# Grouped expert rows in eight slots of 256 and three of 128, instead of eleven of 256

## What is computed

```python
macro_scores = sigmoid(xf @ macro_w)                 # 2048 x 4 groups
mv, mi = topk_normalized(macro_scores, 1)            # one group per row
micro_scores = sigmoid(einsum('td,gde->tge', xf, micro_w))
uv, ui = topk_normalized(micro_scores, 2)            # both experts of the group
w = (macro_full[:, :, None] * micro_full).reshape(T, 8)
gate = silu(einsum('td,edf->tef', xf, gate_w))       # d 256 -> f 512
up = einsum('td,edf->tef', xf, up_w)
out = einsum('te,tef,efd->td', w, gate * up, down_w)
x = x + out
```

## Time and profile before

| | us |
|---|---|
| median of 3 runs (1137.84 to 1138.3) | 1138.0 |
| profiled execution | 1138.74 |
| its span | 1137.0 |
| PE busy | 1035.9 (91%) |
| DVE busy | 783.1 (69%) |
| ACT busy | 692.4 (61%) |
| POOL busy | 565.8 (50%) |
| first h_tb matmul of the experts | at 940.8 |
| last scatter issued | at 1130.4 |

### The profile page before, as it was taken

One profiled execution on the slowest core, in us unless ns is written; L12 is line 12 of the kernel. 1 busy time (PEld: TensorE's weight loads), 2 busy tenths in 40 slices (PEclk: granted clock), 3 DMA queues, 4 the chain that ended last, 5 costly groups with the idle time before them and its releaser, 6 DMA issues. The chain is left out here.

```text
span 1137.0 us, 29115 instructions
## 1 busy us (share of the span) xinstructions
PE 1035.9 (91%) x10375; PEld 759.2 (67%) x10376; DVE 783.1 (69%) x2175; ACT 692.4 (61%) x1297; POOL 565.8 (50%) x685
## 2 busy tenths in 40 slices
PE   6999999999999999984699997898888858999995
PEld 3666777777777777773388884445454447888885
DVE  5887887788778877878734327877777774555452
ACT  6888876787668876757554335476756634334331
POOL 4678644666556553301467826266766432333312
PEclk9999999999999999995799998999999978999998
DMA  8633333343344334307746553534444221111200
GB/s 262 165 85 94 85 77 76 75 88 85 55 103 95 81 80 92 74 16 267 242 153 197 149 126 131 191 97 131 132 123 141 85 98 34 30 34 26 33 10 11
DMA packets 124382, 117.25 MB, mean 103 GB/s; under 512 B 47840, under 2 KB 104416, under 8 KB 124128
## 3 DMA queue, kind: packets, MB, share of 16 engines
q1 hardware_dynamic: 116960, 106.32, 33.5%
q0 software_dynamic: 7296, 9.25, 4.8%
HBM read 59.89 MB, written 21.82 MB: 72 GB/s over the span
## 5 line engine op out<-in xcount | busy, mean ns | idle before, releaser
L810 DVE TENSOR_TENSOR e_t_lo<-et,e_t_hi 128x512 f16<-128x512 f32 x256 | 176.7, 690 | 45.7 <-ACT e_t_hi L697 43.4
L704 ACT ACTIVATE e<-masked,neg_max 128x512 f32<-128x512 f32 x256 | 184.4, 720 | 37.6 <-DVE neg_max L836 35.0
L836 DVE CUSTOM_DVE_ANT_0 masked<-sc,mask_bias 128x512 f32<-128x512 f32 x256 | 175.5, 686 | 31.0 <-issue 26.5
L697 ACT ACTIVATE e_t_hi<-et 128x512 f16<-128x512 f32 x256 | 151.6, 592 | 71.4 <-PE et L581 70.1
L581 PEld LDWEIGHTS et<-ident,e 128*128 128x128 f32 x1024 | 124.5, 140 | 56.7 <-issue 8.7
L581 PE MATMUL et<-ident,e 128*128 128x128 f32 x1024 | 154.4, 273 | 1.0 <-ACT e L704 0.8
L2317 ACT ACTIVATE d_e<-d_st 128x384 f32<-128x384 f32 (+1 forms) x192 | 94.0, 526 | 42.9 <-PE d_st L2461 38.4
L74 PE MATMUL ob<-v_hi,e_t_hi 128*128 128x65 f16 x1024 | 119.0, 193 | 1.2 <-issue 1.2
L75 PE MATMUL ob<-v_lo,e_t_hi 128*128 128x65 f16 x1024 | 119.2, 193 | 0.0
L76 PE MATMUL ob<-v_hi,e_t_lo 128*128 128x65 f16 x1024 | 118.4, 193 | 0.0
L74 PE MATMUL h_hb<-h_xt_hi,experts_hi 128*128 128x256 f16 x352 | 96.8, 275 | 2.1 <-DVE h_xt_lo L2694 1.5
(11 more groups left out here) (504 smaller groups left out, 2847.7 us busy)
## 6 DMA issues: line engine op xcount, KB each, us to landing
kk<-nat_k SPq DMA_DIRECT2D x64, 256.0 KB, 3.5
raw<-in_fc SPq DMA_DIRECT2D x16, 1024.0 KB, 7.6
qq<-nat_q SPq DMA_DIRECT2D x64, 128.0 KB, 2.6
qk<-scratch_stack SPq DMA_DIRECT2D x64, 128.0 KB
scratch_stack<-kq_hi SPq DMA_DIRECT2D x16, 256.0 KB, 2.8
scratch_stack<-kq_lo SPq DMA_DIRECT2D x16, 256.0 KB, 3.0
d_expert_raw<-in_gate_w SPq DMA_DIRECT2D x8, 512.0 KB, 3.7
d_expert_raw<-in_up_w SPq DMA_DIRECT2D x8, 512.0 KB, 3.8
```

Of the source, the lines that this page charges most:

```text
L697: nc.scalar.activation(e_t[u % NBUF].hi[:], et[u % 2][:], ACT.Copy).then_inc(turned_hi, 1)
L704: nc.scalar.activation(e[u % NBUF][:], masked[u % NBUF][:], ACT.Exp, bias=neg_max[:, g % 2, j:j + 1], scale=-1.0).then_inc(exp_ok, 1)
L810: nc.vector.tensor_tensor(e_t[u % NBUF].lo[:], et[u % 2][:], e_t[u % NBUF].hi[:], ALU.subtract).then_inc(turned_lo, 1)
L836: nc.vector.tensor_tensor_reduce(masked[u % NBUF][:], sc[j % 2][:], mask_bias[g // PAIRS % 2][:, j % QT, :], -SCALE0, 3e38, ALU.add, ALU.m ...
```

## The change

Eleven slots stay eleven, but only slots 0 to 7 hold 256 rows (`FULL1` = 8); slots 8, 9 and 10 hold 128. `HALF_TILES`, the number of lists of 128 rows, is 2 * 8 + 3 = 19 instead of 22. A group's rows fill pairs of halves, and a remainder of at most 128 rows goes to a single half; where the pairs are nine, the ninth takes two of the single slots. The search works this out on DVE. In slots 8 to 10 every tile, matmul, activation, gather and scatter is for 128 rows.

```diff
-HALF_TILES = TILES1 * TILE // P
+FULL1 = B * S // TILE
+TILES1 = FULL1 + GROUPS1 - 1
+HALF_TILES = 2 * FULL1 + GROUPS1 - 1
...
-            step_done(dve, nc.vector.tensor_tensor(lower, full.rearrange("p a b -> p (a b)").unsqueeze(1).to_broadcast([P, GROUPS1, GROUPS1 * THRESHOLDS]),
...
-            step_done(dve, nc.vector.tensor_reduce(first_tile, lower, AX.X, ALU.add))
...
+            step_done(dve, nc.vector.tensor_reduce(counts, full.rearrange("p g (k t) -> p k g t", k=2), AX.X, ALU.add))
+            step_done(dve, nc.vector.tensor_tensor(counts[:, SINGLE, :], counts[:, SINGLE, :], counts[:, PAIRED, :], ALU.subtract))
...
+            step_done(dve, nc.vector.tensor_reduce(starts.rearrange("p a k -> p (a k)"), lower, AX.X, ALU.add))
+            pair_start, pair_end = (starts[:, i:i + GROUPS1, PAIRED] for i in range(2))
+            ahead(nc.vector.tensor_scalar(overfull, starts[:, GROUPS1, PAIRED:PAIRED + 1], float(B * S + TILE), float(TILE), ALU.is_ge, ALU.mult))
...
+            step_done(dve, nc.vector.tensor_tensor(over, place, pair_end.unsqueeze(1).to_broadcast([P, NT, GROUPS1]), ALU.is_ge))
...
+            step_done(dve, nc.vector.tensor_tensor(over, over, move.unsqueeze(1).to_broadcast([P, NT, GROUPS1]), ALU.mult))
+            step_done(dve, nc.vector.tensor_tensor(place, place, over, ALU.add))
...
+def halves_of(j):
+
+    return 1 if isinstance(j, int) and j >= FULL1 else 2
...
-            with eng.Fori(0, TILES1 // 2 - 1) as m:
+            with eng.Fori(0, FULL1 // 2 - 1) as m:
...
+            for j in range(FULL1 - 1, TILES1):
+                first(j, j % 2)
+                if j + 1 < TILES1:
+                    turn(j + 1, (j + 1) % 2)
+                tail(j - 1, (j - 1) % 2)
+            tail(TILES1 - 1, (TILES1 - 1) % 2)
...
-                        pool.wait_ge(stored, 32 * j)
+                        pool.wait_ge(stored, 16 * half_at(j))
                         pool.sem_inc(res_free, 1)
-                    for n in range(2):
...
+                    for n in range(halves_of(j)):
...
-                                mm = three_products(pe, hb[g % 2][:, which, :], weights(base, expert * EXPERT_COLS + start + c * FF1 + f * P, P),
-                                                    (xt[i].hi[:, c, :], xt[i].lo[:, c, :]), c == 0, c == DT - 1)
+                                mm = three_products(pe, hb[g % 2][:, which, rows_of], weights(base, expert * EXPERT_COLS + start + c * FF1 + f * P, P),
+                                                    (xt[i].hi[:, c, rows_of], xt[i].lo[:, c, rows_of]), c == 0, c == DT - 1)
```

More of the change, by code:

```diff
@@ L1927, in __init__ @@
         parts, weights = first.take([NT, PER_GROUP, GROUPS1]), first.take([NT, PER_GROUP])
-        full, lower = first.take([GROUPS1, THRESHOLDS]), first.take([GROUPS1, GROUPS1 * THRESHOLDS])
-        first_tile = first.take([GROUPS1])
+        full, counts = first.take([GROUPS1, 2 * THRESHOLDS]), first.take([2, GROUPS1])
+        lower, starts = first.take([2 * (GROUPS1 + 1), GROUPS1]), first.take([GROUPS1 + 1, 2])
+        overfull, fourth, single_at, move = first.take([1]), first.take([GROUPS1]), first.take([GROUPS1]), first.take([GROUPS1])
+        over = first.take([NT, GROUPS1])
         past, tile_group = first.take([TILES1, GROUPS1 - 1]), first.take([TILES1])
+        first_single, past_single = first.take([GROUPS1 - 1]), first.take([TILES1 - FULL1, GROUPS1 - 1])
+        single_group, in_pair = first.take([TILES1 - FULL1]), first.take([TILES1 - FULL1])
         place_at, low_digit, high_digit = (first.take([NT], I32) for _ in range(3))
@@ L1939, in __init__ @@
         ones, tri, zeros = third.take([P], F16), third.take([P], F16), third.take([NT + 1, GROUPS1], F16)
-        order, thresholds, tiles = third.take([GROUPS1]), third.take([THRESHOLDS]), third.take([TILES1])
-        before = third.take([GROUPS1, GROUPS1, THRESHOLDS])
-        ids, low_digits, high_digits = third.take([NT]), third.take([P], F16), third.take([HALF_TILES], F16)
+        order, thresholds, tiles = third.take([GROUPS1]), third.take([2, THRESHOLDS]), third.take([TILES1])
+        before = third.take([GROUPS1 + 1, 2, GROUPS1])
+        ids, low_digits, high_digits = third.take([NT]), third.take([P], F16), third.take([HALF_TILES + 1], F16)[:, 0:HALF_TILES]
         logit = st[2][:, 0:NT * LOGITS1].rearrange("p (t e) -> p t e", e=LOGITS1)
@@ L2102, in search @@
[L2102 to L2104 removed]
+            step_done(dve, nc.vector.tensor_tensor(full, prefix[:, NT, :].unsqueeze(2).to_broadcast([P, GROUPS1, 2 * THRESHOLDS]),
+                                                   thresholds.rearrange("p k t -> p (k t)").unsqueeze(1).to_broadcast([P, GROUPS1, 2 * THRESHOLDS]), ALU.is_gt))
@@ new lines, in search @@
+            step_done(dve, nc.vector.tensor_reduce(counts, full.rearrange("p g (k t) -> p k g t", k=2), AX.X, ALU.add))
+            step_done(dve, nc.vector.tensor_tensor(counts[:, SINGLE, :], counts[:, SINGLE, :], counts[:, PAIRED, :], ALU.subtract))
+            step_done(dve, nc.vector.tensor_tensor(lower.rearrange("p (a k) b -> p a (k b)", k=2), before.rearrange("p a k b -> p a (k b)"),
+                                                   counts.rearrange("p k g -> p (k g)").unsqueeze(1).to_broadcast([P, GROUPS1 + 1, 2 * GROUPS1]), ALU.mult))
@@ new lines, in search @@
+            step_done(dve, nc.vector.tensor_tensor(place, prefix[:, 0:NT, :], pair_start.unsqueeze(1).to_broadcast([P, NT, GROUPS1]), ALU.add))
+            ahead(nc.vector.scalar_tensor_tensor(out=single_at, in0=starts[:, 0:GROUPS1, SINGLE], scalar=overfull, in1=fourth, op0=ALU.add, op1=ALU.add))
+            step_done(dve, nc.vector.tensor_tensor(over, place, pair_end.unsqueeze(1).to_broadcast([P, NT, GROUPS1]), ALU.is_ge))
+            step_done(dve, nc.vector.scalar_tensor_tensor(out=move, in0=single_at, scalar=float(B * S), in1=pair_end, op0=ALU.add, op1=ALU.subtract))
@@ L2680, in first_layer @@
                             act.wait_ge(h_ok, j * HT + (g + 1))
-                            nc.scalar.activation(silu[g % 2][:], hb[g % 2][:, 0, :], ACT.Silu).then_inc(silu_ok, 1)
+                            nc.scalar.activation(silu[g % 2][:, rows_of], hb[g % 2][:, 0, rows_of], ACT.Silu).then_inc(silu_ok, 1)
                         if g >= 1:
@@ L2736, in turn @@
                     pe.wait_ge(xt_lo, j + 1)
-                    pe.wait_ge(rows_in[i], (j - i) * 16 + 32)
-                    for n in range(2):
+                    halves = halves_of(j)
+                    pe.wait_ge(rows_in[i], (j - i) * 16 + 32 if halves == 2 else FULL1 * 16 + ((j - FULL1) // 2 + 1) * 16)
+                    for n in range(halves):
                         for c in range(DT):
@@ L2744, in first_layer @@
                     base = expert_base(j)
+                    rows_of = slice(0, halves_of(j) * P)
                     if begin == 0:
```

74 lines of the change are left out of this document (43 added, 31 removed).

## The result

The kernel now takes 1126.2 us (median of four runs, 1124.5 to 1126.9) where it took 1138.15 (four runs beside them, 1137.8 to 1138.6): a ratio of 0.9892, with a 95% interval of 0.9875 to 0.991. The profiled execution took 1126.0 us, its span 1124.3 against 1137.0. The forecast was 1125.0.

The account below looks back on a forecast made before the run. It took the experts as bound by PE, the search by DVE's small steps, the end by POOL's two scatters. Terms 1.3 - 7.3 + 0.8 - 5.1 + 0.6 - 3.3 = -13.0 gave 1125.0 us, range 1119.5 to 1131.5.

Parts of the forecast that it names:

- search: Route search on DVE: more chained steps, less a smaller largest step and narrower PE list, net +1.3 us.
- firsts of slots 8, 9, 10: PE's first() in the short slots: 8.0 us each, -7.3 in all, plus 0.8 for slots 8 and 9.
- tails 8 and 9: PE's tail(8) and tail(9): half as many matmuls, saving 2.5 + 2.6 = 5.1 us.
- joints: Passages from first() to the next tail: the sequencer loses its lead over PE, together +0.6 us.
- end, from tail(9)'s end: From tail(9)'s last matmul to the span's end: 13.1 us instead of 16.5, -3.3 with rounding.
- The six steps for tile_group: Search on DVE: an estimated 0.8 us, hidden in DVE's 0.91 us wait for PE before expert_weight.
- the sequencer: Short first(): two register instructions make each triple last 0.25 us, so first() takes 8.0 us; the pace chosen.
- the chain: Short first(): PE, silu and product through two PSUM banks take 1.62 us per two blocks, first() 6.5 us.
- The addend of 0.4 for slots 8 and 9: Start of first(8) and first(9): DVE's four tail operations delay the first product, 0.4 us each.
- Rival 1: Short first(): the sequencer keeps up and the two-bank pace holds, 1120.0 us; chance 0.25.
- rival 2: Short first(): the sequencer is slower there than in tail(), first() saves nothing, 1131.5 us; chance 0.13.
- Rival 3: Short slots: PE pauses and its clock falls to 1.2 GHz from first(8) on, 1144 us; chance 0.03.

Follow-up runs that it names:

- constant addresses: Changed kernel with first() of slots 8 to 10 reading group 0's weights from constant columns, without register instructions or tile_group load: 1120.1 us, ratio 0.9834.
- tail(9) earlier: Changed kernel with its last steps reordered to tail(8), tail(9), first(10), tail(10): 1125.73 us, ratio 0.9869; run again, 1125.64 us, ratio 0.9875.
- kept registers: Changed kernel with tails of slots 7 to 10 reusing the register loaded by the same slot's first(): 1124.57 us, ratio 0.9864.

## Why the prediction was right

By its own steps, from the two traces:

| step | predicted | measured |
|---|---|---|
| search | +1.3 | +1.28 |
| firsts of slots 8, 9, 10 | -7.3 + 0.8 | -2.02 - 2.17 - 2.37 = -6.56 |
| tails 8 and 9 | -5.1 | -2.49 - 2.54 = -5.03 |
| joints | +0.6 | -0.25 + 0.42 + 0.30 + 0.45 = +0.92 |
| end, from tail(9)'s end | -3.3 | -3.38 |
| untouched parts | 0 | +0.52 - 0.45 |
| sum | -13.0 | -12.7 |

That the two untouched parts cancel is luck: in the eleven experiments' profiles their sum lies between 1.9 under and 2.5 over that of the kernel before. Of the 1.2 us between the forecast of 1125.0 and the median of 1126.2, 0.3 is this sum, and 0.9 is that I put the median 0.7 below the profiled execution, as it was in the kernel before, where it lay 0.2 above it.

**The search.** The group cost 1.55 (1.6 said) and the largest step gave back 0.19 (0.2 said). Counted from the search's first reduce, gather_at comes 1.47 later than before, expert_weight 1.11, and the first matmul of first(0) 1.28; why 0.17 is lost behind expert_weight no run shows. The six steps for tile_group did fall into the wait for PE: from the largest step to expert_weight it is 2.72 us, 3.07 before. But I wrote that expert_weight would still wait, and it doesn't. That matters for the next edit: in the chain of waits the experts' start hangs on DVE entering their block, 1.5 us after the end of expert_weight (1.3 before),

```profile
942.30 0.03 DVEq L2761
942.33 0.28 issue
942.61 1.10 PE h_tb L2784 x4
```

so that a seventh step should have no cover left; this was not tried.

**first().** The choice of the sequencer over the chain, made from two tail starts, was the one that mattered, and it is shown: with the register instructions first(10) takes 7.9 to 8.0 us whether the banks are two or three, and without them 5.9. My 6.5 for the chain was too high. It is four times 1.62, but from the first start to the last only three waits lie; three times 1.62 and the last pair's 1.27 make 6.1. The rest is that two blocks took 1.54, not 1.62. That slots 8 and 9 came to 6.6 is no confirmation, since 0.7 of it is the late first product. The addend of 0.4 for slots 8 and 9 had the right size (measured 0.35 and 0.20) for half the reason. I charged the late product and forgot the sequencer's lead behind a full tail; the one costs 0.7 to 1.0 (by the two runs that remove it), the other saves 0.6 to 0.7 (8.0 against 7.37 and 7.28). For the time it made no difference; for what to do next it does, since it hid 1.4 us that a reordering gives back.

**Tails** went as counted. From tail(8)'s start to first(10)'s it is 2.75, predicted 2.76: eight triples at 0.25 and the load. Without first(10)'s load (constant addresses) it is 2.63, PE's own pace for 24 of these matmuls.

**Joints** are the term that was mis-sized: 1.06 and 1.08 before tail(7) and tail(8), where I had 0.99, 0.88 before tail(9), where I had 0.79, and the joint before tail(7) had been 0.64 in the kernel before, not the 0.78 that I took from tail(8) for both the earlier trace rows. I had read one row and used it twice. The row that I did not read, PE of the kernel before around the transposes of tail(7)'s start:

```profile
1081.98 0.27 PE L76 MATMUL h_hb<-h_xt_hi,experts_lo 128*128 128x256 f16 x1
...
1082.62 0.28 PE L74 MATMUL h_ob<-experts_hi,h_hs_hi 128*128 x1
```

**The end** held: 13.1 us from tail(9)'s end, predicted 13.1. Its parts held as well: 1.9 to scatter(9)'s issue (1.92 said), 4.7 from there to scatter(10)'s (4.5 said), 6.5 to the span's end (6.6 said).

**The rivals.** Rival 1 (the sequencer keeps up) and rival 2 (slower in first()) are excluded by first(10)'s 8.0 us. Rival 3, the clock, did not come in the changed kernel, where PE's idle times in the short slots are 0.8 us or less. The run with tail(9) earlier shows that it is no idle fear: one pause of 1.46 us, and the last tail took 1.6 us longer. The Trainium skill, page "TensorE: Matmul & The Clock Gate", section "A second HAM failure mode: psum-queue depth-cycling", expects such a fall from small idle times between groups that cycle PSUM banks; with constant addresses and two banks PE had such pauses (1097.46 to 1097.71 above) and the clock stayed at 1.00, so these traces do not bear it out for short pauses; the one fall that they show came behind a single long one.

The Trainium skill, page "TensorE: Matmul & The Clock Gate", section "Back-to-back issue gap", has 81 ns for a matmul of 128 columns in a stream of loads and matmuls, an estimate of 7.8 us for first(). That is close to what was measured, but the agreement is luck: without register work the spacing is 0.056.

## What to carry to other kernels

When an edit halves the columns of a matmul, ask what stays the same per instruction: here two register instructions a triple, hidden under 0.327 us, became the pace at 0.25, so that half the work gave 23% less time in first(). The place to read such a pace before the edit is where the engine starts after a pause. A cover (idle time that hides added work) is spent once: check what of it is left. And a small effect is best read as a distance inside a trace, between two events that lie around it, when the rest of the program scatters by more.

## What the runs showed of the hardware

- The clock fell to 0.50 for some 3.4 us behind a pause of PE of 1.46 us (tail(9) earlier: 0.51 over 1111 to 1114, 1.00 before and from 1114.5 on), and in a second profile of the same kernel, behind a pause of 1.46 again, it did not.
- Behind a full tail of 256-column matmuls the narrow ones start at PE's own pace although their register instructions are there: two blocks at 0.056 a matmul with two PSUM banks, three with three banks, and then 0.083. Behind a half tail (first(10) of the changed kernel) no block does. That the sequencer has got ahead of PE by then is the reading; no row shows it directly.
- Two register instructions make a triple of 128-column matmuls last 0.25 us (8.00 for 32) instead of PE's own 0.167 (5.30 for 32): L76's load stands 0.08 behind L75's, and the next L74's 0.14 behind that. Loading such a register from tile_group, with the instructions that follow it, cost 0.65 to 0.71 at the three joints (kept registers).
